# Attention and experts in one kernel: row copies by two engines, zeros on another queue, query and key parts stored once and read twice

## The reference

```python
x = L0_attn_x                                    # (8, 512, 256)
xn = _layernorm(x, axis=-1)
# attention: 16 heads of 16, causal, with ALiBi slopes
kqv = xn @ W_kqv + b_kqv
attn = softmax(q @ k^T / sqrt(16) + slopes * tril(j - i), masked above the diagonal)
y = (attn @ v) @ W_proj + b_proj
# eight experts; each takes its 512 best tokens, a token goes to one expert
probs = softmax(xn @ Wg); tok2exp = ...          # top_k per expert, then argmax
h = gelu(xn @ W1[e]) @ W2[e]                     # for the expert e of the token
return x + y + probs[tok2exp] * h
```

## Time and profile before

| | us |
|---|---|
| median of 3 runs | 688.47 |
| lowest and highest | 686.81, 691.18 |
| the profiled execution | 688.02 |
| its span, first to last instruction | 686.2 |
| TensorE busy in it | 561.0 |
| VectorE busy in it | 413.5 |
| ScalarE busy in it | 331.1 |
| GpSimd busy in it | 328.5 |

### The profile page before, as it was taken

How to read it: one execution, slowest core, us unless ns; L and a number is a source line. 1 busy time by engine, 2 the same in 40 slices (tenths; PEclk the granted TensorE clock), 3 DMA queues, 4 the chain that set the end, 5 groups by cost and what they waited for, 6 DMA issues and landing times.

```text
span 686.2 us, 13215 instructions
## 1 busy us (share of the span) xinstructions
PE 561.0 (82%) x4515; PEld 334.7 (49%) x4515; DVE 413.5 (60%) x819; ACT 331.1 (48%) x623; POOL 328.5 (48%) x481
## 2 busy tenths in 40 slices
PE   1878488648888989989975979998887989999992
PEld 0445254324334534535433534545333878787782
DVE  4655435959999688797798688585322333333331
ACT  3454454207665565555652456575664333333330
POOL 5647110303444354343441338787863277655552
PEclk9999799959999999999998999999999999999997
DMA  4698787591323151241421135353488445654310
GB/s 138 188 255 119 238 279 258 189 278 56 110 64 102 57 171 55 86 139 55 142 86 54 57 116 156 115 174 101 124 288 288 89 117 136 120 109 110 93 48 8
DMA packets 100671, 92.12 MB, mean 134 GB/s; under 512 B 36658, under 2 KB 89843, under 8 KB 100599
## 3 DMA queue, kind: packets, MB, share of 16 engines
q1 hardware_dynamic: 90336, 69.69, 36.2%
q0 software_dynamic: 6576, 17.91, 8.6%
q10 hardware_dynamic: 3696, 3.67, 2.0%
HBM read 44.22 MB, written 40.05 MB: 123 GB/s over the span
## 4 chain that ended last, share of the span: by engine, by line
PE 40%; DVE 26%; POOL 12%; issue 10%; ACT 5%; DMA 4%; SPq 2%; POOLq 0%; DVEq 0%; ACTq 0%
DVE mx L849 11%; PE ps L1248 10%; PE ps L1261 7%; PE ps L1056 7%; PE ps L1152 6%; POOL sorted_rows L582 4%; PE ps L1138 4%; POOL pr_all L605 3%; DVE mx L844 3%; PE ps L1127 2%; PE ps L1108 2%; POOL yn L579 2%; POOL w_low L572 2%; ACT pr_all L663 2%; DVE thr L907 1%
## 5 line engine op out<-in xcount | busy, mean ns | idle before, releaser
L735 ACT ACTIVATE pr_all<-ps 128x512 f32<-128x512 f32 x320 | 180.9, 598 | 178.0 <-PE ps L1127 176.7
L849 DVE TENSOR_REDUCE mx<-ps 128x2 f32<-128x768 f32 (+1 forms) x192 | 156.9, 859 | 42.0 <-PE ps L1108 41.2
L605 POOL TENSOR_SCALAR_AFFINE_SELECT pr_all<-pr_all 128x384 f32<-128x384 f32 x128 | 64.5, 529 | 177.1 <-ACT pr_all L735 177.1
L1127 PE MATMUL ps<-qs,ks 128*128 128x512 f16 (+2 forms) x448 | 116.0, 332 | 15.7 <-ACT pr_all L735 7.0
L1108 PE MATMUL ps<-ks,qs 128*128 128x384 f16 (+3 forms) x512 | 116.9, 314 | 0.0
L1105 PE MATMUL ps<-maxmask,idb 128*128 128x256 bf16 (+1 forms) x320 | 84.3, 263 | 33.1 <-DVE mx L849 19.4
L1138 PE MATMUL ps<-pr_all,vt 128*17 128x512 f32 (+3 forms) x1024 | 87.4, 461 | 4.8 <-POOL pr_all L608 4.7
L1152 PE MATMUL ps<-wp,yn 128*128 128x256 f32 x256 | 69.8, 399 | 14.3 <-DVE xr L874 8.0
L1248 PE MATMUL ps<-pr_all,xnp 128*128 128x128 f16 x936 | 77.4, 223 | 0.2
L1127 PEld LDWEIGHTS ps<-qs,ks 128*128 128x128 f16 x448 | 38.3, 100 | 74.8 <-ACT pr_all L735 41.4
L1023 DVE TENSOR_TENSOR pr_all<-pr_all 128x512 f16<-128x512 f32 x39 | 27.3, 703 | 77.4 <-ACT pr_all L749 75.1
(11 more groups left out here) (174 smaller groups left out, 793.7 us busy)
## 6 DMA issues: line engine op xcount, KB each, us to landing
qs<-q_parts SPq DMA_DIRECT2D x64, 100.0 KB
ks<-k_parts SPq DMA_DIRECT2D x64, 96.0 KB
sorted_rows<-ecmp POOLq DMA_DIRECT2D x1, 5160.0 KB, 22.9
k_parts<-pr_all SPq DMA_DIRECT2D x16, 256.0 KB, 3.1
q_parts<-pr_all SPq DMA_DIRECT2D x16, 256.0 KB, 2.8
xr<-in_L_attn_x_dram SPq DMA_DIRECT2D x8, 512.0 KB, 4.2
w_h<-in_L_ffn_W_dram SPq DMA_DIRECT2D x16, 256.0 KB, 3.4
w_l<-in_L_ffn_W_dram SPq DMA_DIRECT2D x16, 256.0 KB, 3.9
```

Of the source, the lines that this page charges most:

```text
L605: pool.affine_select(out=v, in_=v, compare_op=ALU.is_ge, fill=0.0, base=0, pattern=[[0, 3], [1, P]], channel_multiplier=-1).then_inc(sel_m ...
L735: act.activation(dst, src, ACT.Exp, scale=SCORE).then_inc(exp_made, 1)
L849: last = dve.tensor_reduce(mx[:, n1 % 2, :, 2 * g + c, t], ps[:, 2 * (u % 2):2 * (u % 2) + 2, c0:c0 + w], AX, ALU.max)
L1127: last = pe.matmul(out, ks[:, p, c, t * P:(t + 1) * P], rhs, start=True, stop=True, skip_group_check=True)
```

## The change

ScalarE copies only the high half of the turned rows, after all four `hi` (except for the very first rows), and VectorE copies the low half after its four subtractions. The five transfers of `zero_rows` are issued by ScalarE, in n = 1 between its fourth `hi` and its row copy. `constant_rows` moves from n = 2 to n = 3 and `alibi_rows` from n = 4 to n = 5. Each k or q result is stored with one transfer (32 rows of `k_parts` or `q_parts` instead of 48), and the loads read the high block a second time: eight transfers a group, for each half of the partitions k with 32 and 16 rows, q with 16 and 34 (two blocks and the zero rows).

```diff
-    qk_d = [... for n, r in (("k", ROWS), ("q", QROWS))]
+    qk_d = [... for n, r in (("k", 2 * D), ("q", 2 * D + 2))]
...
             def load_group(n, g):
                 p, cs = n % 2, slice(2 * g, 2 * g + 2)
                 for e in range(2):
-                    for dst, src in ((ks[HALF * e + R_DATA:HALF * e + R_SHIFT, p, cs], qk_d[0]),
-                                     (qs[HALF * e + R_DATA:HALF * e + R_FREE, p, e, cs], qk_d[1])):
-                        v = src[n, g // 2].rearrange("r (c e n) -> r e c n", e=2, n=S)
-                        sp.dma_start(dst, v[:, e, 2 * (g % 2):2 * (g % 2) + 2, :]).then_inc(grp_in[p][g], 16)
+                    r0, hi = HALF * e + R_DATA, slice(0, D)
+                    for dst, r1, r2, src, rows in ((ks, 0, 2 * D, qk_d[0], slice(0, 2 * D)), (ks, 2 * D, ROWS, qk_d[0], hi),
+                                                   (qs, 0, D, qk_d[1], hi), (qs, D, QROWS, qk_d[1], slice(0, 2 * D + 2))):
+                        v = src[n, g // 2, rows].rearrange("r (c e n) -> r e c n", e=2, n=S)
+                        to = dst[r0 + r1:r0 + r2, p, cs] if dst is ks else dst[r0 + r1:r0 + r2, p, e, cs]
+                        sp.dma_start(to, v[:, e, 2 * (g % 2):2 * (g % 2) + 2, :]).then_inc(grp_in[p][g], 16)
 
             def store_parts(n, c):
                 sp.wait_ge(lo_made, 4 * n + c + 1)
-                both, again = ((0, 2), (1, 0))[c // 2]
-                v = qk_d[c // 2][n, c % 2, :, :]
-                sp.dma_start(v[both * D:(both + 2) * D].rearrange("(s d) (h n) -> (d h) s n", s=2, n=S),
-                             pt[n % 2][c]).then_inc(parts_out[n % 2][c], 16)
-                sp.dma_start(v[again * D:(again + 1) * D].rearrange("d (h n) -> (d h) n", n=S),
-                             pt[n % 2][c][:, 0, :]).then_inc(parts_out[n % 2][c], 16)
+                v = qk_d[c // 2][n, c % 2, 0:2 * D, :]
+                sp.dma_start(v.rearrange("(s d) (h n) -> (d h) s n", s=2, n=S), pt[n % 2][c]).then_inc(parts_out[n % 2][c], 16)
...
             for n in range(B):
-                if n == 1:
-                    zero_rows()
-                if n == 2:
+                if n == 3:
                     constant_rows()
-                if n == 4:
+                if n == 5:
                     alibi_rows()
...
             def take_rows(n):
                 act.wait_ge(t_made, n + 1)
                 after(act, v_made, 4 * (n - 1))
-                for a_ in range(2):
+                for a_ in range(1 if n else 2):
                     act.activation(xt[n % 2][:, a_]...)
+
+            def zero_rows():
+                act.wait_ge(const_made, 11)
+                ...                                # the same five transfers, now act.dma_start
...
                 for c in range(4):
                     hi(c)
-                    if n < B - 1 and c == 2:
-                        take_rows(n + 1)
+                if n == 1:
+                    zero_rows()
+                if n < B - 1:
+                    take_rows(n + 1)
...
+                if n < B - 1:                      # VectorE, after its four subtractions
+                    dve.wait_ge(t_made, n + 2)
+                    after(dve, v_made, 4 * n)
+                    dve.tensor_copy(xt[(n + 1) % 2][:, 1].rearrange("p k n -> p (k n)"), bank[1].bitcast(F16)).then_inc(t_used, 1)
```

More of the change, by code:

```diff
@@ L98, in layer @@
     x_t = x.rearrange("b (t p) e -> b p t e", p=P)
-    qk_d = [nc.dram_tensor(f"{n}_parts", [B, 2, r, NP * S], F16, kind="Internal").ap() for n, r in (("k", ROWS), ("q", QROWS))]
+    qk_d = [nc.dram_tensor(f"{n}_parts", [B, 2, r, NP * S], F16, kind="Internal").ap() for n, r in (("k", 2 * D), ("q", 2 * D + 2))]
     xa_d = nc.dram_tensor("x_plus_attention", [T, E], F32, kind="Internal").ap()
@@ L304, in _ @@
             sp.dma_start(wp[D:D + 1, 0, :], b_proj[None, :]).then_inc(cst_in, 16)
[L306 to L313, removed]
             def constant_rows():
@@ L372, in _ @@
                     for c in range(4):
-                        sp.wait_ge(parts_out[r][c], 32)
+                        sp.wait_ge(parts_out[r][c], 16)
                     for g in (0, 1) if n % 2 else (2, 3):
@@ L377, in _ @@
                 for c in range(4):
-                    sp.wait_ge(parts_out[p][c], 32 * B // 2)
+                    sp.wait_ge(parts_out[p][c], 16 * B // 2)
             load_x(0)
@@ L661, in take_rows @@
                 after(act, v_made, 4 * (n - 1))
-                for a_ in range(2):
+                for a_ in range(1 if n else 2):
                     act.activation(xt[n % 2][:, a_].rearrange("p k n -> p (k n)"), bank[a_].bitcast(F16),
                                    ACT.Copy).then_inc(t_used, 1)
+            def zero_rows():
+                act.wait_ge(const_made, 11)
+                for p in range(2):
+                    for e in range(2):
+                        act.dma_start(qs[HALF * e:HALF * (e + 1), p, 1 - e],
+                                      empty[HALF * e:HALF * (e + 1), 0:S][:, None, :].broadcast_to([HALF, NP, S])
+                                      ).then_inc(zeros, 16)
+                act.dma_start(qk_d[1][:, :, 2 * D:2 * D + 2, :].rearrange("b a r m -> (b a) (r m)"),
+                              empty[0:2 * B, 0:S][:, None, :].broadcast_to([2 * B, 2 * NP, S])).then_inc(zrows_in, 16)
             for n in (1, 2):
@@ L686, in hi @@
                     act.wait_ge(qk_made, 4 * n + c + 1)
-                    after(act, parts_out[n % 2][c], 32 * (n // 2))
+                    after(act, parts_out[n % 2][c], 16 * (n // 2))
                     act.activation(pt[n % 2][c][:, 0, :], bank[2 + c], ACT.Identity, bias=bqk[:, c:c + 1]).then_inc(hi_made, 1)
@@ L1097, in max_unit @@
                 if k == 0:
-                    pe.wait_ge(grp_in[p1][g], 64 * (n1 // 2 + 1))
+                    pe.wait_ge(grp_in[p1][g], 128 * (n1 // 2 + 1))
                 after(pe, max_made, u - 1)
```

## The result

| | before | after |
|---|---|---|
| median, us | 687.66 (4 runs) | 698.09 (4 runs) |
| ratio to before, 95% interval | | 1.0126 (1.0102 to 1.0150) |
| span of the profiled execution | 686.2 | 695.7 |
| stage's last copy | 111.95 | 114.14 |
| SP issues `load_x(0)` | 116.98 | 132.47 |

The changed kernel is slower by 1.3%. The forecast was 685.6, slightly faster, with a range up to 694. The whole difference is there by the first score: 9.0 of the 9.5 us of span. Behind it both kernels keep step (the last exponential of the middle part starts at 536.97 instead of 528.22, 8.75 us later). Three of the four runs of the kernel before are those of the table ahead of the prediction.

What follows compares the result with a forecast made beforehand. The first stage and SP's issues there were taken as the bound. Stage terms summed to -6.9 us, most given back behind it by SP's +8.0 at `load_x(0)`; total -2.4 gave 685.6 us, range 676 to 694 (forecast's own 681 to 689).

Steps and rivals of the forecast that it cites:

- Row copies: First stage, copies shared by ScalarE and VectorE: 1.55 us saved per period, -10.9 over seven turns; VectorE's copy 1.1, hidden.
- Zeros: Five transfers on ScalarE's queue at n = 1 hold it 6.0 us (2.7 to 8.35); TensorE restarts 5.2 later.
- Clock: After TensorE sits still 5 to 6 us behind the zeros, the lower clock adds 1.5 us (0 to 1.6).
- Two queues: First stage's 34-row q loads use two DMA engines: 10.6 us of work an iteration against a 9.18 period.
- rival A: Loads of 34 rows spread well and SP's issue time bounds instead: stage end -10.6, 678 us; chance 0.18.
- Constants: Issued one iteration later: old stall at n = 4 goes, -8.8 us; drain 20.7, only +0.3 remains at n = 5.
- Landing of `shift_rows`: Behind the stage, with the fill 1.4 us ahead instead of 7.4: takes 8.0 us, 149.7 instead of 152.1.
- Rival B: Two engines slower than 0.047 us a packet, for instance 0.075: `shift_rows` lands about 165, 701 us; chance 0.13.
- Rival C: Landing of `shift_rows` gains nothing, as the fill and SP's delay cancel the stage's gain: 688 us; chance 0.16.

Runs made afterwards that it cites:

- the first run: Kernel before with only the row copies changed (ScalarE the high half after its four hi, VectorE the low half): ratio 0.982.
- zeros back: Changed kernel with the five zero transfers issued by SP again, at the start of n = 1: ratio 0.996.
- the run with the zeros apart: Changed kernel with the five zero transfers still on ScalarE's queue but issued singly behind second and fourth hi over n = 0 to 2: ratio 0.998.

## Why the prediction was wrong, step by step

The first score moved by +9.0, and the runs divide it: row copies -7.4 (the first run), later constants and alibi +0.7, parts +7.0 (zeros back against row copies with later constants), zeros on ScalarE's queue +8.7 (changed against zeros back). The sum is +9.0, as it must be, each share being the difference of two neighbours. The shares hold in this order; the +0.7 is within what two executions differ by, and the parts alone, with SP's slack untouched, cost 1.0.

*Row copies: right.* Forecast 1.55 a period, measured 10.73 - 9.24 = 1.49. VectorE's copy took 0.68, below the 1.1 taken, and is hidden.

*Zeros: the step that failed.* I bounded the hold by 2.7 and 8.35 and took 6.0, because ScalarE's queue would be nearly empty. It was 9.34 (43.92 - 34.58), above my upper bound. The third, fourth and fifth transfers took 2.57, 2.77 and 2.46, and on SP they had taken 2.28, 2.27 and 2.26 (with the two before them 6.04 and 2.26 in the earlier trace rows): they blocked here as there. Beside them ran four stores of SP, between 32.2 and 36.4, on the same engines, and the DMA share was 0.95 from 34.5 to 44. The empty queue was no reason: the first two issues of the burst cost 0.7 each on either queue, and the run with the zeros apart shows that the rest are dear only when they find those two undrained. The upper bound was a row taken under other traffic and should have been widened.

*Clock: right in kind, short in size.* I added 1.5; the granted clock was 0.50 from 44 to 50, and 36 matmuls took 8.96 instead of 6.70, +2.26. The first iteration's 24 matmuls, too, took 8.22 in the changed kernel against 7.22 in the kernel before; the first period of the other runs with the row copies was 9.5 to 10.9, so this differs between executions; I take it for the low clock of the start, which no run isolates. Together the head of n = 2 stood at 50.7 instead of 45.6: +5.1.

*Two queues: right.* Loads of 34 rows go by two engines: the slice with share 0.13, the 0.95 once they are split, and 8.6 us back with 50 rows (fewer issues included). By the rule in the Trainium skill, page "DMA: Bandwidth & Descriptors", section "Why a DMA increments its semaphore by 16 and not by 1" (the largest number up to 16 that divides the slowest dimension), 34 rows get two engines. The runs agree with it. The rival A falls.

*Constants: too short.* `load_x(0)` was forecast at 125.0 and came at 132.5. Of these 7.5 us 5.1 are the head of n = 2. The heads of n = 3 and 4 stayed as late (60.0 and 69.2 instead of 54.8 and 63.9), that of n = 5 was 8.5 late (84.0 instead of 75.5), the end of the stage 8.9 (114.14 instead of 105.2), and 1.4 were made good behind it. So the next 3.2 us arose at the wait for the store behind the constants: from the first constant to its end I had 24.0 us (51.5 to 75.5), and it was 27.4 (56.59 to 84.02). Which part of the drain took longer no run separates; in the other runs that issue the constants in one piece the same stretch was 25.3 to 30.0. VectorE's slow normalising in n = 3 (3.76 us instead of 1.38, while GpSimd spread the slopes over `qs` for 7.24 us from 61.61) did not delay the head of n = 4.

*Landing of `shift_rows`: wrong by 3.8.* I took 8.0 between unhindered 4.9 and full 12.4, since the fill led by 1.4 us instead of 7.4. It was 11.8: a lead of 1.4 us is enough. Unhindered it is 3.8. Here two ends were known and the middle was taken without a row near it; the fill itself landed 22.4 us after its issue, so both leads put the four transfers well inside it.

The two lots of lateness, 7.5 and 3.8, added to the forecast first score of 149.7 give 161.0; it was 161.15. Rival B had the right sign and size but the wrong cause: the two engines were not slower per packet than assumed (0.045 us by the slice above); what SP waited for had been started late. Rival C had the landing of `shift_rows` gain nothing; it did worse and came 9.0 us later. The missing case was the one where the zeros hold ScalarE longer than on SP. As SP has no slack left behind the doubled loads, most of it goes through to the end (with the zeros back on SP the head of n = 2 was 11.1 us earlier and the first score 8.7), and with the 5.1 us of that head alone my own sum would have stood at 690.7, slower than before.

## What to carry to other kernels

A burst of five transfers on ScalarE's queue held it for the drain of all but the first two: with such a burst on a computing engine's queue, spread the burst over iterations, or leave it on a queue that only issues (spreading won 3 us over that on the changed kernel and lost 3.2 on the kernel before), and price it with the traffic of the other queues in the same window. Count the rows of each transfer before splitting it: 50 rows went by ten engines, 34 by two, and storing a third fewer bytes did not pay for that. When a stage is made faster, look at the queue behind it for slack first, and take nothing from it in the same step.

## What the runs showed of the hardware that was not expected

- Five transfers of 2304 rows of 1 KB in sum held ScalarE 9.3 us in one burst and 3.3 us with 2.6 us or more from one start to the next; apart, beside the kernel before's twice as many stores, their traffic slowed half of SP's store issues from 0.5 to between 2 and 3 us each.
- A fill of 5.16 MB issued 1.4 us ahead made four 8 KB transfers land 11.8 us after their first issue instead of 3.8, nearly as much as with a lead of 7.4 us (12.4).
- VectorE copied 128x1024 fp16 values out of PSUM in 0.68 us, where ScalarE took 1.02 for as many and a VectorE reduction over as many fp32 columns 1.21.
- VectorE's four 256-column normalisations took 3.76 us instead of 1.38 beside a 7.24 us cast on GpSimd, and 4.95 in the run with the zeros back on SP; no run takes the cast away.
